# A gated cross- and self-attention block on one core: the self-attention mixed features first, and two tiles' similarity placed by TensorE

## What is computed

```python
x = x + tanh(g_xattn) * cross_attention(layernorm(x), ctx_1024, ctx_1024)
# second layer, of layernorm(x):
q, k, v = (x @ W_qkv) in 16 heads
sim = (guide_unit * q[:, 5:] / norm(q[:, 5:])).sum(-1).mean over heads
sim = (sim - sim.min()) / (sim.max() - sim.min())      # over all batches
pos = sim > 0.9
# masked_attn(m): softmax over the 5 registers and the tokens with m, then the product with v
x_pos, x_neg = masked_attn(pos), masked_attn(~pos)
registers = (x_pos[:, :5] + x_neg[:, :5]) * 0.5
tokens = where(pos, x_pos[:, 5:], x_neg[:, 5:])
x = x + tanh(g_ffn) * (concat(registers, tokens) @ W_proj + b_proj)
```

## Time and profile before

| | us |
|---|---|
| median of 3 runs | 2613.17 (2612.43 to 2616.61) |
| profiled execution | 2608.9, of which the span is 2607.1 |
| `stage_rows` ends, self block begins | 2257.45 |
| TensorE busy in the span | 2504.7 (96%) |
| mean granted TensorE clock | 0.975 |

### The profile page before, as it was taken

One profiled execution on the slowest core, in us unless ns is written; L12 is line 12 of the kernel. 1 busy time (PEld: TensorE's weight loads), 2 busy tenths in 40 slices (PEclk: granted clock), 3 DMA queues, 4 the chain that ended last, 5 costly groups with the idle time before them and its releaser, 6 DMA issues. The chain is left out here.

```text
span 2607.1 us, 47776 instructions
## 1 busy us (share of the span) xinstructions
PE 2504.7 (96%) x17376; PEld 2271.7 (87%) x17376; DVE 1804.5 (69%) x2869; ACT 1332.0 (51%) x3000; POOL 384.0 (15%) x281
## 2 busy tenths in 40 slices
PE   7899999999999999999999999999969999699999
PEld 6889999999999999999999999999848888588887
DVE  7467777777777777777777777777757666456665
ACT  3344555555555545555555555455534444355554
POOL 0311111111111111111111111111124333000000
PEclk9999999999999999999999999999869999789999
DMA  7645545555545555455554555544469999899993
GB/s 224 204 119 134 124 124 128 128 132 127 130 122 129 131 129 135 113 130 130 131 128 121 127 131 128 128 130 116 108 165 209 207 202 197 184 180 189 188 184 82
DMA packets 324830, 379.91 MB, mean 146 GB/s; under 512 B 126332, under 2 KB 232220, under 8 KB 324636
## 3 DMA queue, kind: packets, MB, share of 16 engines
q1 hardware_dynamic: 322772, 375.80, 61.4%
q10 hardware_dynamic: 1864, 1.43, 0.2%
HBM read 162.57 MB, written 72.57 MB: 90 GB/s over the span
## 5 line engine op out<-in xcount | busy, mean ns | idle before, releaser
L740 DVE TENSOR_TENSOR c_parted<-c_prob,c_parted 128x600 fp32r<-128x600 f32 x512 | 400.7, 783 | 363.3 <-ACT c_prob L686 363.3
L864 PE MATMUL c_mix<-c_parted,c_v 120*66 120x200 f32 (+1 forms) x3072 | 544.7, 270 | 0.7 <-DVE c_parted L740 0.6
L849 PEld LDWEIGHTS c_pair<-c_q_stack,c_k_stack 100*120 100x120 f32 (+1 forms) x3072 | 517.5, 186 | 10.9 <-issue 6.3
L849 PE MATMUL c_pair<-c_q_stack,c_k_stack 100*120 100x100 f32 (+1 forms) x3072 | 519.9, 227 | 6.3 <-DVE c_parted L740 5.0
L726 DVE TENSOR_REDUCE c_peak<-c_pair 100x1 f32<-100x724 f32 x512 | 456.6, 907 | 55.2 <-PE c_pair L811 39.8
L682 ACT ACTIVATE c_parted<-c_pair 128x600 fp32r<-128x600 f32 x512 | 344.4, 673 | 283.6 <-PE c_pair L849 283.4
L864 PEld LDWEIGHTS c_mix<-c_parted,c_v 120*66 120x66 f32 (+1 forms) x3072 | 418.2, 140 | 3.1 <-DVE c_parted L740 0.9
L686 ACT ACTIVATE c_prob<-c_pair 128x600 f32<-128x600 f32 x512 | 341.8, 668 | 0.0
L664 ACT ACTIVATE c_v<-c_work 120x512 fp32r<-120x512 f32 (+1 forms) x192 | 115.6, 602 | 442.4 <-PE c_work L91 442.4
L811 PE MATMUL c_pair<-c_k_stack,c_q_stack 96*100 96x362 f32 x1024 | 254.2, 329 | 0.0
L1657 ACT ACTIVATE s_prob<-s_scores,s_shift 106x100 f32<-106x100 f32 x512 | 169.6, 363 | 136.1 <-DVE s_shift L1690 136.1
(11 more groups left out here) (200 smaller groups left out, 5296.1 us busy)
## 6 DMA issues: line engine op xcount, KB each, us to landing
c_k_stack<-c_k_hi SPq DMA_DIRECT2D x1024, 90.2 KB, 2.1
e_stage<-in_ctx SPq DMA_DIRECT2D x32, 1444.0 KB, 6.4
c_k_stack<-c_k_lo SPq DMA_DIRECT2D x512, 90.2 KB, 2.1
c_q_stack<-q_parts SPq DMA_DIRECT2D x192, 100.0 KB, 2.4
mix_parts<-w_mixed SPq DMA_DIRECT2D x64, 200.0 KB, 3.2
r_parts<-mix_parts SPq DMA_DIRECT2D x22, 512.0 KB, 7.5
s_q_stack<-qk_parts SPq DMA_DIRECT2D x10, 800.0 KB
s_k_stack<-qk_parts SPq DMA_DIRECT2D x10, 800.0 KB
```

The costliest lines, as they stand in the source:

```text
L740: dve.tensor_tensor(p[:, :, 1, :], prob[i % 2][:], p[:, :, 0, :], ALU.subtract).then_inc(p_lo_done, 1)
L849: return pe.matmul(pair[i % 2][0:r, t // (CT // 2), col:col + S], k_stack[:, i, c_cols(t)], q_stack[:, i, :], start=True, stop=True)
L864: return pe.matmul(mix[g % 2][0:VW, at * 2 * S:(at + 1) * 2 * S], v[0:r, t, i, :], parted[i % PR][0:r, t, :, :].rearrange("p a s -> p (a s)"),
```

## The change

**Similarity.** The columns of the last two tiles (23 and 24) no longer go through memory. The first 23 tiles are loaded back (in two transfers, onto a cleared tile) by ScalarE between its steps for tiles 23 and 24. The two last columns are reduced into two zeroed tiles `placed` of 34 columns, and TensorE places them by four products with the identity (`place_similarity`), between the projections of tile 24 and the turning of its q and k. VectorE adds the result and takes the batches' ends ahead of `split_qk(24)`, the rest of the tables after it.

**Mixing.** Stationary are now the values of a head (100 x 32), moving is `pt` (100 x 106), so the result has features on partitions: four heads fill four strips of 32 partitions of one bank, `out_bank` of two in turn, in which the projection of the batch stands afterwards. `fold_mix`, `weigh`, the constant `fold` and its load are gone. The registers' two columns are joined by two small VectorE instructions ahead of the split (20 columns each). The inverse sums are applied to the probabilities before they are turned: VectorE inverts quarter by quarter, POOL multiplies (`scale`, 106 x 400, four a batch), and `turn_probs` waits for that. All copies to `pt` are VectorE's; ScalarE has the exponentials alone. POOL's register copies stand in its one stream behind the scales of each odd batch. SP's start of the block has the second pair ahead of the values of batch 1 and of x1.

```diff
+        self.placed = [m.sb(f"placed{i}", [P, B + PLACED]) for i in range(PLACED)]
...
-                if t < TILES - 1:
+                if t < TILES - PLACED:
...
+                if t == TILES - 2:
+                    pool.wait_ge(cross_w.mix_stored, 48 * B)
+                    pool.memset(begin.sim, 0.0).then_inc(begin.sim_clear, 1)
...
             split_qk(TILES - 2)
+            for i in range(2):
+                act.wait_ge(sim_stored[i], 16 * ((TILES - PLACED + 1 - i) // 2))
+            act.wait_ge(begin.sim_clear, 1)
+            whole, rest = divmod((TILES - PLACED) * P, S)
+            act.dma_start(begin.sim[0:whole, :], sim_dram[0:whole * S, :].rearrange("(b s) a -> b (s a)", s=S)
+                          ).then_inc(begin.sim_in, 16)
+            act.dma_start(begin.sim[whole:whole + 1, 0:rest],
+                          sim_dram[whole * S:whole * S + rest, :].rearrange("(b s) a -> b (s a)", s=rest)
+                          ).then_inc(begin.sim_in, 16)
             queries(TILES - 1, True)
             query_root(TILES - 1)
             keys(TILES - 1)
-            act.wait_ge(sim_ready, TILES)
-            act.dma_start(sim_dram[(TILES - 1) * P:TILES * P, :], sim[(TILES - 1) % 2][:]
-                          ).then_inc(sim_stored[(TILES - 1) % 2], 16)
             values(TILES - 1)
             split_qk(TILES - 1)
-            for i in range(2):
-                act.wait_ge(sim_stored[i], 16 * ((TILES + 1 - i) // 2))
-            act.wait_ge(cross_w.mix_stored, 48 * B)
-            act.dma_start(begin.sim, sim_dram.rearrange("(b s) a -> b (s a)", s=S)).then_inc(begin.sim_in, 16)
             act.wait_ge(begin.tables_ready, 1)
...
+                if t >= TILES - PLACED:
+                    dve.wait_ge(begin.placed_clear, PLACED)
+                    to = begin.placed[t - (TILES - PLACED)][:, B - 1:B]
...
+            def ends_of_batches(step):
+                dve.wait_ge(begin.sim_in, 32)
+                dve.wait_ge(begin.sim_placed, 1)
+                dve.tensor_tensor(begin.sim, begin.sim, ends_bank[0:B, PLACED_AT:PLACED_AT + S], ALU.add).then_inc(begin.sim_joined, 1)
+                dve.wait_ge(begin.sim_joined, 1)
...
+            def place_similarity():
+                pe.wait_ge(sim_ready, TILES)
+                for t in range(TILES - 1, TILES - 1 - PLACED, -1):
+                    for b in range((t * P + P - 1) // S, t * P // S - 1, -1):
+                        lo, hi = max(t * P, b * S), min(t * P + P, b * S + S)
+                        column = begin.placed[t - (TILES - PLACED)][:, B - 1 - b:2 * B - 1 - b]
+                        last = pe.matmul(ends_bank[0:B, PLACED_AT + lo - b * S:PLACED_AT + hi - b * S], column,
+                                         ident[:, lo - t * P:hi - t * P], start=(b == B - 1), stop=(lo == (TILES - PLACED) * P))
+                last.then_inc(begin.sim_placed, 1)
...
             project_all(TILES - 1, True)
+            place_similarity()
             turn_qk(TILES - 1)
...
             load_values(0, 0)
-            sp.dma_start(fold[:], fold_dram.rearrange("e q s -> q e s")).then_inc(fold_in, 16)
+            sp.wait_ge(cleared, 2 * (STACKS - 1))
+            load_pair(2, 1)
             load_values(1, 1)
             load_x1(0, 0)
-            sp.wait_ge(cleared, 2 * (STACKS - 1))
-            load_pair(2, 1)
             load_x1(1, 1)
...
+            def scale(b, odd, j):
+                pool.wait_ge(inv_done, b * HPT + j + 1)
+                quarter = prob[:, j, :, :]
+                pool.tensor_tensor(quarter, quarter,
+                                   repeated(inv[odd][:, j * KT:(j + 1) * KT].unsqueeze(2), 2, S), ALU.mult
+                                   ).then_inc(scaled, 1)
+            for b in range(RING):
+                for j in range(HPT):
+                    scale(b, b % 2, j)
+                if b == 0:
+                    copies(1, 0)
+                elif b % 2:
+                    copies((b + 3) // 2 % STACKS, (b + 3) // RING)
...
-            def invert(b, odd):
-                dve.wait_ge(exp_done, b * HPT + HPT)
-                dve.reciprocal(inv[:], total[odd][:]).then_inc(inv_done, 1)
+            def invert(b, odd, j):
+                dve.wait_ge(exp_done, b * HPT + j + 1)
+                dve.reciprocal(inv[odd][:, j * KT:(j + 1) * KT], total[odd][:, j * KT:(j + 1) * KT]).then_inc(inv_done, 1)
...
-            def weigh(b):
+                                ).then_inc(pt_done, 1)
+            def split_mix(b, odd):
+                mixed = out_bank[odd][:, 0:KT * QR].rearrange("p (k q) -> p k q", k=KT)
+                rows, copies = (0, S) if odd else (SIDE, 0)
+                tokens, registers = mixed[:, :, rows:rows + S], mixed[:, :, rows:rows + REG]
                 dve.wait_ge(mix_full, b + 1)
-                dve.wait_ge(inv_done, b + 1)
-                dve.tensor_tensor(mixed[:].rearrange("p (m a d) -> p m a d", a=HPT, d=HD),
-                                  mix_bank[0:QR, :].rearrange("p (m a d) -> p m a d", a=HPT, d=HD),
-                                  repeated(inv[:].rearrange("p (a m) -> p m a", m=KT).unsqueeze(3), 3, HD),
-                                  ALU.mult).then_inc(mixed_done, 1)
-            def split_mix(b):
-                folded = proj_bank[:, 0:KT * S].rearrange("p (k s) -> p k s", k=KT)
-                dve.wait_ge(o_turned, b + 1)
-                dve.tensor_copy(ot_hi[:], folded).then_inc(ot_hi_done, 1)
+                dve.tensor_scalar(seconds[:], mixed[:, :, copies:copies + REG], 0.5, None, ALU.mult).then_inc(folded, 1)
+                dve.wait_ge(folded, 2 * b + 1)
+                dve.scalar_tensor_tensor(registers, registers, 0.5, seconds[:], ALU.mult, ALU.add).then_inc(folded, 1)
+                dve.wait_ge(folded, 2 * b + 2)
+                dve.tensor_copy(ot_hi[:], tokens).then_inc(ot_hi_done, 1)
                 dve.wait_ge(ot_hi_done, b + 1)
-                dve.tensor_tensor(ot_lo[:], folded, ot_hi[:], ALU.subtract).then_inc(ot_lo_done, 1)
+                dve.tensor_tensor(ot_lo[:], tokens, ot_hi[:], ALU.subtract).then_inc(ot_lo_done, 1)
...
                 turn_back(b, 0)
                 if not last:
                     shift_of(b + 1, 0)
+                invert(b, odd, 3)
                 turn_back(b, 1)
                 if not last:
                     shift_of(b + 1, 1)
                 if before:
-                    split_mix(b - 1)
-                invert(b, odd)
+                    split_mix(b - 1, 1 - odd)
+                turn_back(b, 2)
                 if not last:
                     shift_of(b + 1, 2)
+                    invert(b + 1, 1 - odd, 0)
                 turn_back(b, 3)
                 if not last:
                     shift_of(b + 1, 3)
+                    invert(b + 1, 1 - odd, 1)
                 if before:
                     stores = (pair if odd else pair - 1) if before > 2 else None
                     result(b - 1, 1 - odd, (i - 1) % DEEP, deep if i % DEEP else deep - 1, stores)
-                weigh(b)
+                if not last:
+                    invert(b + 1, 1 - odd, 2)
...
-                pe.wait_ge(exp_done, b * HPT + n + 1)
+                pe.wait_ge(scaled, b * HPT + n + 1)
...
-            def mix(b, n, at):
+            def mix(b, odd, n, at, deep):
+                pe.wait_ge(pt_done, b * HPT + n + 1)
+                if n == 0:
+                    pe.wait_ge(v_in[at], 16 * deep + 16)
                 for k in range(KT):
                     cols = slice((k * HPT + n) * HD, (k * HPT + n + 1) * HD)
-                    last = pe.matmul(mix_bank[0:QR, cols], pt[:, n * KT + k, :], values[at][:, cols],
-                                     start=True, stop=True)
+                    last = pe.matmul(out_bank[odd][n * HD:(n + 1) * HD, k * QR:(k + 1) * QR], values[at][:, cols],
+                                     pt[:, n * KT + k, :], start=True, stop=True)
                 if n == HPT - 1:
                     last.then_inc(mix_full, 1)
-            def fold_mix(b, odd, follows=True):
-                pe.wait_ge(mixed_done, b + 1)
-                if follows:
-                    pe.wait_ge(y_ready, b)
-                for k in range(KT):
-                    last = pe.matmul(proj_bank[:, k * S:(k + 1) * S], mixed[:, k * P:(k + 1) * P], fold[:, odd, :],
-                                     start=True, stop=True)
-                last.then_inc(o_turned, 1)
...
                 if before:
-                    pe.wait_ge(pt_act, b)
+                    pe.wait_ge(pt_done, b * HPT - 1)
                 turn_probs(b, 0)
                 if not last:
                     score(b + 1, at, 0, step + (i + 1) // RING)
                 if before:
-                    pe.wait_ge(pt_dve, 3 * b)
+                    pe.wait_ge(pt_done, b * HPT)
                 turn_probs(b, 1)
                 if not last:
                     score(b + 1, at, 1, step)
-                if before:
```

(26 more changed lines are left out.)

101 lines of the change are left out of this document (44 added, 57 removed).

## The result

The changed kernel takes 2596.07 us (2594.36 to 2598.11), the kernel before 2614.55 in the same session: a ratio of 0.993 (95% interval 0.9912 to 0.9947), 18.5 us faster. I had forecast 5.4 faster, 2607.8, and a range down to 2600.5. The direction was right, the size was not, and the likeliest time lies 11.7 us above the measured one.

The account below looks back on a forecast made before the run. The prediction took the self stage as bound by its pair loads (20.05 us a pair against TensorE's 19.5). Terms -5.2 + 1.9 - 2.1 = -5.4 from the median 2613.17 gave 2607.8 us, range 2600.5 to 2617.5.

Parts of the forecast that it names:

- The similarity, 5.2: End of the rows stage: without the similarity's store and reload the self block begins at 2252.2, 5.2 us gained (4.1 to 6.5).
- The body's period, 9.52: Self stage: TensorE's body without load waits takes 9.52 us against 9.75, fold gone but a new wait added.
- the new wait for VectorE: In each self-stage body TensorE stands 0.94 us (0.6 to 1.0) before the projection, until VectorE has joined and split the registers.
- its reading of L818: One trace case of a 4-column stationary: at most 0.09 for two loads and a switch, so switching tiling mode costs nothing seen.
- rival C: Self stage: mixing costs 0.12 an instruction or switches drain 0.2 each, or similarity is held up; 2611 to 2617, chance 0.18.
- rival B: Self stage: loads not late, or mixing cheap at 0.051 an instruction; 2600 to 2605, chance 0.22.
- While loads run the 0.23 are hidden by them: Self stage: the 0.23 us a body gains nothing while pair loads run; it counts only in bodies 28 to 30, 0.7.
- Part 3, the loads 2.3 late: POOL's order delays body 2, so loads from pair 4 on run 2.3 us late (0 to 4); 1.9 lost at body 28.
- The end, 2.1: After the last load: bodies 28 to 30 gain 0.7, body 31 0.3, the work behind the last mixing 1.1.
- D: Self stage: the new wait in each body lowers TensorE's clock to a mean of 0.92, period 10.3; 2621, chance 0.15.

Follow-up runs that it names:

- self stage alone: Only the self stage of the change, with the rows stage and similarity of the kernel before: 2606.45 us, ratio 0.9963 to the kernel before.
- the second profile of before: The unchanged kernel before, profiled again: this execution took 2624.77 us, with TensorE at half clock until past 2330.

## Why the prediction was wrong

**The similarity, 5.2:** right in its steps but not in its base. The tables were ready at 2246.88 for 2246.1, the block began 0.8 earlier than forecast, inside the ends (of which the earlier one should have been 2246.1 + 3.7 = 2249.8, not 2250.8). But the 8.8 us for the small store came from one execution; others show 9.8 to 12.4, and the part is worth 8.0. This was the first failed step: a landing time in a loaded queue, read once, was taken as its price.

**The body's period, 9.52:** 9.23 to 9.26. The mechanism was right, the new wait for VectorE stood where it was worked out. Two terms were too large: a mixing instruction (0.086, was 0.0775) and the small VectorE instructions (0.25 apart, were 0.21). Against it stood 9.75, from one body without a hitch; over 27 bodies the old one takes 9.81. The difference is 0.57 instead of 0.23.

The prediction set its reading of L818, that a switch between wide and narrow products costs nothing, against rival C's drain of 0.2. The starts of single instructions show a cost between the two. From the last scoring product to the first mixing one it is 0.187 in the changed kernel, body after body, and 0.093 where mixing followed scoring in the kernel before; from a projection's last product to the first mixing one 0.326 against 0.233; from the last mixing product to the next turning 0.182 against 0.093. So each change of width added 0.09, and the two around the last two quarters stand in the period in full, 0.18 of the 9.23. The Trainium skill, "TensorEngine Tiling (Array Packing)", section "Key Properties", says that changing the tiling mode drains TensorE. The 0.09 agree with that, though no run here isolates the drain. The group is cheaper than forecast all the same, because at the join of its two quarters several instructions start 0.01 to 0.06 apart instead of 0.09.

The Trainium skill, "Perfetto Trace Analysis", section "Engine Utilization", halves the output rate for full 32-bit products; for 106 columns at half of 2.4 GHz that is an estimate of 0.088. A mixing product is two instructions here and took 0.155, an instruction 0.0775. Taken for an instruction, the 0.088 is above what was measured. Taken for the product it is below, and then it does not exclude rival B's 0.051 an instruction, as the prediction had it. What excludes the 0.051 is the measured price.

**"While loads run the 0.23 are hidden by them":** the step on which the prediction failed. It was read from the spacing of issues, 20.05, against 19.5 for two bodies, and from four short waits. The comparison was too fine for one profile: in others of the old stage TensorE never waits for a load and paces them, at 265.0 for 27 bodies. And waits for loads lost more than their length, so that the old stage took 6.7 us for 3.7 us of waits. In the place of a fixed pace the runs show two near limits, TensorE's 265.0 and the loads', with the clock between them. The changed body moves one of them to 249.6, well under the loads'. It takes 260.2 to 263.4 in the three profiles with the loads as they were made, so 5.5 us against the old stage's average are gained there, where the forecast had 0.7.

**Part 3, the loads 2.3 late:** half right. SP issued pair 4 56.6 behind the block's begin, where before it was 54.2: 2.35 late, as worked out. That body 4 came at the forecast place was luck in part: body 2 began 1.2 earlier than forecast, but lost 4.2 to the clock and not 2.3. Yet the pair landed 76.1 behind it, before 76.5. I had argued that nothing covers the delay, from the share of 0.72 and the landing of pair 3; it was covered all the same, and by what stays open. And body 28 began at 2548.87, by the forecast 2554.2: 0.8 from the begin, 5.7 from pair 15, which landed earlier than the fixed pace and the delay allowed, less 1.2 for a longer way from its landing to the body.

**The end, 2.1:** 5.4 in the profiles, 3.3 more. Of these 0.8 come from the shorter bodies (1.5 for 0.7 over three), and 1.5 from the clock at the last projection, which fell in all five profiles of the old self stage and stayed up in six of eight of the new. The forecast had no term for it. The waits before it are near to one another (2.1 for the fold and the split before, 1.7 now). The remaining 1.0 is in body 31 and in the instructions behind the last mixing.

**The rivals.** B (2600 to 2605) was on the right side and named two of the causes, the loads not late and cheaper mixing (0.051 as its bound, 0.0775 measured), but not the largest, the 27 bodies. Its support was misread: at the projection's rate the columns of eight products of turning and scoring need 0.40 (an estimate from 1.48 / 6 for 512), and they took 0.715. C's price of 0.12 didn't show, and of its drain less than half did, 0.09. D, the clock lowered by the new wait of each body, didn't come: with 0.74 of waiting in every body the windows have a granted clock of 1.00,

```profile
2310.00:2320.00 10.00, 9.26 (x89) 7.53 (x85) 7.32 (x20) 6.30 (x38) 3.89 (x6) 1.00 1.11 193
```

while waits for a load were followed by a fall in some cases and not in others. The length of the single wait does not tell them apart: waits of 0.69 (before, at 2318.24) and 0.86 (before with lighter loads) were followed by one, waits of 1.0 to 1.1 (changed kernel with copies late, at 2474, 2493 and 2512) and of 1.36 (self stage alone, at 2458.89) were not. What does was not tested.

## What to carry to other kernels

Where two limits lie within 3% of each other, as TensorE's 19.6 and the loads' 20.1 a pair, one profile doesn't tell which binds; look for the sum over many bodies without a wait (265.0) and ask what each limit alone would give, before an edit is counted as hidden. An engine with slack against its loads can also make up for what went wrong at the start (with the copies late, 11 us at body 4 were nothing at body 31), and one without it carries it to the end (the second profile of before). And look at the DMA share within a period: the loads with few partitions, put first instead of last, were worth as much as half of the whole change.

## What the runs showed of the hardware

- What a short wait of TensorE costs by the clock varied widely: 3.7 us of waits made the bodies around 10.4 us longer in the changed kernel, one wait of 0.86 was followed by 20.5 us at half clock and 10.0 us lost in the kernel before with lighter loads, and one of 1.36 was followed by no fall in the self stage alone. 0.74 us in every body of 9.25 left the clock at 1.00.
- 32 stationary and 106 moving columns in full 32-bit cost 0.0775 us an instruction in groups of 16, 106 stationary and 32 moving columns 0.086: turning the product round cost nothing, though it moves three times the columns. Each change between such products and those of the full width added 0.09 us.
- A store of 0.5 KB behind large stores took between 8.8 and 12.4 us to land in five executions of the same code.
